# Sampling through the offsets phase: a gather table held twice, and six sample groups moved out of the first deform tiles

## What is computed

```python
x = x + _L0_conv_ref(_gn(x), ...)   # chunked linear attention, then group norm
x = x + _L1_conv_ref(_gn(x), ...)   # 3x3 conv gives per-pixel offsets; bilinear resampling; 3x3 conv
x = x + _L2_conv_ref(_gn(x), ...)   # 3x3 convolution
x = x + _L3_conv_ref(_gn(x), ...)   # deformable 3x3 convolution
```

## Time and profile before

| | us |
|---|---|
| median of 3 runs (11071.03 to 11081.85) | 11077.26 |
| profiled execution, span from first to last instruction | 11438.4 |
| mean granted TensorE clock in it, share of full | 0.775 |
| POOL busy, share of span | 6270.5 (55%) |
| PE busy, share | 6712.3 (59%) |
| DVE busy, share | 6213.1 (54%) |
| ACT busy, share | 2154.2 (19%) |

### The profile page before, as it was taken

The page is one execution under the profiler, slowest core; times in us unless marked ns, Lnnn a source line. Parts: engine busy times, 40 slices in busy tenths (PEclk is TensorE's granted clock), DMA queues, the critical chain, the costliest instruction groups (busy, mean ns, idle before and its releaser), DMA issues. The chain is left out here.

```text
span 11438.4 us, 98360 instructions
## 1 busy us (share of the span) xinstructions
PE 6712.3 (59%) x29196; PEld 4294.5 (38%) x29196; DVE 6213.1 (54%) x6833; ACT 2154.2 (19%) x3660; POOL 6270.5 (55%) x5206
## 2 busy tenths in 40 slices
PE   5455777656667677755676595756576583121212
PEld 3223336544454235534454234634454331111111
DVE  6797324566784524466795424466696433333333
ACT  2331311221221311122130221121221130000000
POOL 0000006578776406668876504668876605777777
PEclk8777888878888788877888797878788796555555
DMA  0000112222232312222223212222223222333333
GB/s 25 17 0 17 55 52 84 91 88 87 82 94 79 99 42 91 82 92 87 86 77 95 93 40 95 86 92 86 87 77 97 81 62 77 97 98 97 98 97 90
DMA packets 426636, 878.37 MB, mean 77 GB/s; under 512 B 119692, under 2 KB 250134, under 8 KB 423444
## 3 DMA queue, kind: packets, MB, share of 16 engines
q0 software_dynamic: 248832, 679.81, 20.1%
q1 hardware_dynamic: 174228, 121.56, 3.7%
q10 hardware_dynamic: 3456, 75.50, 1.6%
HBM read 764.88 MB, written 111.60 MB: 77 GB/s over the span
## 5 line engine op out<-in xcount | busy, mean ns | idle before, releaser
L589 POOL DMA_INDIRECT gathered_corners<-gather_table,metas x5184 | 6262.2, 1208 | 5143.2 <-issue 3134.3
L1212 PE MATMUL ps<-ident,weighted_corners 128*128 128x128 f32 (+1 forms) x10800 | 1590.1, 314 | 579.1 <-DVE weighted_corners L646 554.4
L1212 PEld LDWEIGHTS ps<-ident,weighted_corners 128*128 128x128 f32 (+1 forms) x10800 | 1500.6, 216 | 756.3 <-issue 584.9
L1215 PE MATMUL ps<-ident,sampled 128*128 128x128 f32 (+1 forms) x1530 | 370.6, 401 | 2407.1 <-DVE sampled L653 2399.6
L648 DVE TENSOR_TENSOR gathered_corners<-gathered_corners,metas 128x2304 f32<-128x2304 f32 x306 | 783.1, 2559 | 1665.3 <-DMA gathered_corners<-gather_table,metas 1603.8
L1016 ACT COPY sampled_by_channel<-ps 128x512 f32<-128x512 f32 x576 | 337.1, 585 | 5722.1 <-PE ps L1215 2688.5
L1286 PE MATMUL ps<-region,woff 128*128 (+1 forms) x3456 | 1222.7, 511 | 23.6 <-ACT region L1001 23.6
L1215 PEld LDWEIGHTS ps<-ident,sampled 128*128 128x128 f32 (+1 forms) x1530 | 248.2, 194 | 2552.0 <-issue 2438.7
L820 DVE TENSOR_TENSOR work<-work 128x768 f32<-128x768 f32 x960 | 888.3, 953 | 17.1 <-ACT work L1079 11.1
L646 DVE TENSOR_TENSOR weighted_corners<-gathered_corners,metas 128x2304 f32<-128x2304 f32 x270 | 690.9, 2559 | 340.6 <-DMA gathered_corners<-gather_table,metas 186.1
L1286 PEld LDWEIGHTS ps<-region,woff 128*128 128x128 f32 x3456 | 674.8, 199 | 516.2 <-issue 87.5
(11 more groups left out here) (205 smaller groups left out, 7276.9 us busy)
## 6 DMA issues: line engine op xcount, KB each, us to landing
gathered_corners<-gather_table,metas POOLq DMA_INDIRECT x5184
x_after_layer<-region ACTq DMA_DIRECT2D x8, 4608.0 KB, 12.3
gather_table<-tabst SPq DMA_DIRECT2D x192, 192.0 KB, 2.5
region<-in_x_dram ACTq DMA_DIRECT2D x12, 1536.0 KB
region<-x_after_layer ACTq DMA_DIRECT2D x4, 4608.0 KB, 16.6
res<-x_after_layer SPq DMA_DIRECT2D x144, 128.0 KB
out_dram<-ob SPq DMA_DIRECT2D x144, 128.0 KB
indices_and_weights<-region SPq DMA_DIRECT2D x16, 810.0 KB, 4.2
```

The costliest lines, as they stand in the source:

```text
L589: pool.indirect_dma_start(out=G[:, s % NG, k, :], out_offset=None, in_=table, in_offset=bass.IndirectOffsetOnAxis(ap=idx[:, s * KK + k:s * ...
L1212: mm = pe.matmul(out_m, W[:, q, 128 * m:min(128 * m + 128, KK * C)], ident[:, :], start=q == 0, stop=q == 3)
L1215: mm = pe.transpose(out_m, V[:, s % 2, 128 * m:min(128 * m + 128, KK * C)], ident[:, :])
```

## The change

- The table in DRAM is twice as long. Pass p writes the half p % 2 and the sampling of pass p reads the other, so that sampling may go on while the table is written. `first_row` (one number on each partition) holds the base of the indices and is flipped between the halves at the end of each pass. `setup()` zeroes the whole second half with two stores of 98 x 99 rows of 512 bytes each, ahead of the border stores on SP.
- The first six deform tiles carry one group each instead of two, by the schedule of the second six (PLACES[1]).
- The six groups taken away are sampled in the offsets phase: PARTS is 6, a part is 4 tiles and one group. PE does a step behind each tile, DVE weighs the four steps (summing on DVE), then does the part's indices and weights (now on 216 columns), then `finish`. SP's loads and stores of the group stand between the cosine loads, and its stores of the parts' indices and weights (six now) come after the last group's result is stored.

```diff
-PARTS = 4
+PARTS = 6
...
-G_TAPS = (G_NORM + 1, G_NORM + 1 + 12)
+G_TAPS = (G_NORM + 1, G_NORM + 1 + 6)
 G_CONV = (G_TAPS[1] + 6, G_TAPS[1] + 10)
-assert G_CONV[1] + 4 == GROUPS
+G_OFFSETS = G_CONV[1] + 4
+assert G_OFFSETS + PARTS == GROUPS
...
 PLACES = {0: ((), (), (), (), (), ()),
-          1: (((0, 0),), (), ((0, 1),), ((0, 2),), ((0, 3),), ((0, None),)),
-          2: (((0, 0), (0, 1)), ((0, 2),), ((0, 3),), ((0, None), (1, 0), (1, 1)), ((1, 2), (1, 3)), ((1, None),))}
+          1: (((0, 0),), (), ((0, 1),), ((0, 2),), ((0, 3),), ((0, None),))}
...
-DVE_SUMS = {1: (), 2: ((0, 1), (1, 1), (1, 3))}
...
-        table = dram("gather_table", (2 * TAB, 2 * C))
+        table = dram("gather_table", (2 * 2 * TAB, 2 * C))
...
+        first_row = sb("first_row", [128, 1])
...
-            tab4 = table.rearrange("(b h w) c -> b h w c", b=2, h=TAB_H)
+            tab4 = table.rearrange("(b h w) c -> b h w c", b=4, h=TAB_H)
             stores = []
+            for b in (2, 3):
+                stores.append((tab4[b], zero[0:TAB_H, 0:2 * C].unsqueeze(1).to_broadcast([TAB_H, TAB_W, 2 * C])))
...
+                    chain.own(chain.after().memset(first_row[:, :], float(TAB_W + 1)))
...
-            tiles_groups = (2, 1) if sample else (0, 0)
+            tiles_groups = (1, 1) if sample else (0, 0)
...
-            tabp = table.rearrange("(i h w) c -> i h w c", i=2, h=TAB_H)
+            if prepare:
+                tabp = table[bass.ds(p % 2 * (2 * TAB), 2 * TAB), :].rearrange("(i h w) c -> i h w c", i=2, h=TAB_H)
...
+                    sp.dma_start(metas[:, slot, :], meta_before[:, bass.ds(g * META, META)]).then_inc(meta_loaded[slot], 16)
...
+                def load_res(g):
+                    sp.dma_start(res[:, :], x3_before[:, bass.ds(g * GN, GN)]).then_inc(res_loaded, 16)
...
+                def store_out(g):
+                    sp.wait_ge(group_added, g + 2)
+                    sp.dma_start(out_before[:, bass.ds(g * GN, GN)], ob[:, :]).then_inc(out_stored, 16)
...
+                def group(g, e, last=False):
+                    load_res(g)
+                    if not last:
+                        sp.wait_ge(weighted, g * STEPS + CREDIT)
+                        load_meta(g + 1, 1 - e)
+                    store_out(g)
+
                 if sample:
...
+                    ahead = G_OFFSETS if prepare else GROUPS - 2
+                    with sp.Fori(0, ahead // 2) as j:
                         for e in range(2):
-                            group(j * 2 + e, e, False)
...
+                if not prepare:
+                    group(GROUPS - 2, 0)
                     group(GROUPS - 1, 1, True)
...
                     sp.wait_ge(out_stored, 16 * (GROUPS + 1))
-                if not prepare:
                     return
...
-                with sp.Fori(0, RT // 2) as j:
-                    for e in range(2):
...
-                        sp.wait_ge(om_mm, j * 2 + (e + 1))
...
+                def load_cosines(t, e):
+                    sp.wait_ge(om_mm, t + 1)
...
+                for h in range(PARTS):
+                    g = G_OFFSETS + h
+                    for u in range(4):
+                        load_cosines(h * 4 + u, u % 2)
+                        if sample and u == 1:
+                            if h > 0:
+                                store_out(g - 1)
+                            load_res(g)
+                            if g + 1 < GROUPS:
+                                sp.wait_ge(weighted, g * STEPS + CREDIT)
+                                load_meta(g + 1, (g + 1) % 2)
+                if sample:
+                    store_out(GROUPS - 1)
+                    sp.wait_ge(out_stored, 16 * (GROUPS + 1))
                 for h in range(PARTS):
...
-                                if e == 0:
-                                    steps_of(j * 2 + (G_TAPS[0] + gi), (G_TAPS[0] + gi) % 2, (s,), (gi, s) not in DVE_SUMS[2])
-                                else:
-                                    steps_of(j + G_TAPS[1], (j + G_TAPS[1]) % 2, (s,))
+                                steps_of(j + G_TAPS[e], (j + G_TAPS[e]) % 2, (s,))
...
                 with v.Fori(0, PARTS) as h:
+                    steps_of(h + G_OFFSETS, (h + G_OFFSETS) % 2, (0, 1, 2, 3), False)
                     v.wait_ge(om_tcp, h * (RT // PARTS) + (RT // PARTS + 2))
...
-                            ch.own(ch.after().tensor_scalar(idx, fl, float(TAB_W), float(TAB_W + 1), ALU.mult, ALU.add))
+                            ch.own(ch.after().tensor_scalar(idx, fl, float(TAB_W), first_row[:, :], ALU.mult, ALU.add))
...
                     ch.named(ch.after().tensor_tensor(wts[:, :, :, 0], half(q2), half(fl), ALU.subtract), meta_made, h + 1)
+                    steps_of(h + G_OFFSETS, (h + G_OFFSETS) % 2, (None,))
                     ch.restart()
+                ch.own(ch.after().tensor_scalar(first_row[:, :], first_row[:, :], -1.0, float(2 * (TAB_W + 1) + 2 * TAB), ALU.mult, ALU.add))
+                ch.after()
...
-                                steps_of(j * 2 + (G_TAPS[0] + gi) if e == 0 else j + G_TAPS[1], (s,))
+                                steps_of(j + G_TAPS[e], (s,))
...
+                        steps_of(h + G_OFFSETS, (u,))
                     mask(h)
...
+                    steps_of(GROUPS - 1, (u,))
                 mask(PARTS - 1)
...
-                            steps_of(j * 2 + (G_TAPS[0] + gi) if e == 0 else j + G_TAPS[1], (s,), (gi, s) not in DVE_SUMS[2 - e])
+                            steps_of(j + G_TAPS[e], (s,))
...
                 offsets_and_mask(0, 0, 0)
-                with pe.Fori(0, RT // 2 - 1) as j:
-                    offsets_and_mask(j * 2 + 1, 1, j)
-                    turn_offsets(j * 2, 0)
-                    offsets_and_mask(j * 2 + 2, 0, j + 1)
-                    turn_offsets(j * 2 + 1, 1)
-                offsets_and_mask(RT - 1, 1, RT // 2 - 1)
-                turn_offsets(RT - 2, 0)
-                turn_offsets(RT - 1, 1)
+                with pe.Fori(0, PARTS - 1) as h:
+                    for u in range(4):
+                        offsets_and_mask(h * 4 + (u + 1), (u + 1) % 2, h * 2 + (u + 1) // 2)
+                        turn_offsets(h * 4 + u, u % 2)
+                        steps_of(h + G_OFFSETS, (u,), False)
+                for u in range(4):
+                    t = RT - 4 + u
+                    if u < 3:
+                        offsets_and_mask(t + 1, (u + 1) % 2, (t + 1) // 2)
+                    turn_offsets(t, u % 2)
+                    steps_of(GROUPS - 1, (u,), False)
```

More of the change, by code:

```diff
@@ L488, in _, with load_meta @@
             def _(sp):
-                if sample:
[L491 to L500, removed]
+                def load_meta(g, slot):
+                    sp.dma_start(metas[:, slot, :], meta_before[:, bass.ds(g * META, META)]).then_inc(meta_loaded[slot], 16)
[10 more added lines that the diff above has]
+                    store_out(g)
+                if sample:
                     load_meta(0, 0)
-                    with sp.Fori(0, GROUPS // 2 - 1) as j:
+                    ahead = G_OFFSETS if prepare else GROUPS - 2
+                    with sp.Fori(0, ahead // 2) as j:
                         for e in range(2):
-                            group(j * 2 + e, e, False)
-                    group(GROUPS - 2, 0, False)
+                            group(j * 2 + e, e)
+                if not prepare:
+                    group(GROUPS - 2, 0)
                     group(GROUPS - 1, 1, True)
                     sp.wait_ge(out_stored, 16 * (GROUPS + 1))
-                if not prepare:
                     return
@@ L548, in _ @@
                 sp.wait_ge(cst_zeroed, 1)
-                with sp.Fori(0, RT // 2) as j:
-                    for e in range(2):
-                        sp.wait_ge(om_mm, j * 2 + (e + 1))
[L553 to L561, removed]
-                            src = cos_dram[k:k + 1, bass.ds((r0 + 1 - sy) * PAD2 + (1 - sx), run)]
-                            sp.dma_start(cst[e][q:q + 6].rearrange("p h w -> p (h w)"),
-                                         bass.AP(src.tensor, src.offset, [[1, 3], [4 * PAD2 * PAD2, 2], [1, run]])).then_inc(cs_loaded[e], 16)
+                def load_cosines(t, e):
+                    sp.wait_ge(om_mm, t + 1)
+                    r0 = t * ROWS
+                    run = cst[e][0:24].rearrange("p h w -> p (h w)").shape[1]
+                    src = cos_dram[:, bass.ds((r0 + 1) * PAD2 + 1, run)]
+                    sp.dma_start(cst[e][0:24].rearrange("p h w -> p (h w)"),
+                                 bass.AP(src.tensor, src.offset, [[1, 3], [PAD2 * PAD2, 8], [1, run]])).then_inc(cs_loaded[e], 16)
+                    for k, (sy, sx) in enumerate(DIRECTIONS):
+                        q = 24 + k * 6
+                        src = cos_dram[k:k + 1, bass.ds((r0 + 1 - sy) * PAD2 + (1 - sx), run)]
+                        sp.dma_start(cst[e][q:q + 6].rearrange("p h w -> p (h w)"),
```

(2 more changed lines are left out.)

## The result

The changed kernel takes **10492.5 us** (median of four runs, 10487.2 to 10495.9) against 11079.6 us for the kernel before, timed beside it: a ratio of 0.9469, 95% interval 0.9455 to 0.9482. The forecast was 10612 us (0.958), its range 10460 to 10790. The direction and the mechanism held; the gain is a quarter larger than forecast, 587 us where 465 were foreseen. One timed run among all that follow, of the kernel of experiment 8, took 15001 us beside three of 10903 to 10907, and the ratio there leaves it out.

The account below looks back on a forecast made before the run. No engine bounds the whole: POOL is overloaded in the first six deform tiles and idle in the PE-bound offsets phase. 3 x (134 - 300) - 3 + 21 takes 11438 to 10958, scaled to 10612 us; range 10460 to 10790.

Parts of the forecast that it names:

- first six tiles: Deform tiles 0 to 6 of a pass: six intervals fall from 695.0 to 395.2 us, -300 us a pass.
- offsets phase: After the cosines, POOL leads with the moved groups; the phase ends at 4389 instead of 4267.4, +122 us a pass.
- end of the pass: After the last result's store, six stores of indices and weights, 3.3 MB, take 13 us: +12 us a pass.
- setup, once: Zeroing 9.9 MB at 255 GB/s moves the next block's first issue from 60.1 to 81: +21 us, between nothing and +74.
- pass 0's phase, once: Offsets phase of pass 0, which has no sampling: its parts are smaller at the end, -3 us.
- The first part: Offsets phase: PE gives the fourth tile at about 4100, the second group's first weighing ends at 4118; POOL stands 22 us.
- The pace behind it: Offsets phase after the first part's lag: 18 steps x 13.2 + 4 x 3, 250 us, to 4368, ending at 4389.
- the 3 us a part: Offsets phase: DVE's index and weight work, 12.5 us a part, takes 3 us from POOL, making its sum 55.7.
- case 3: Waits between engines add up, index work blocks POOL fully: 65.2 us a group, +173 in the offsets phase; 10761 us; 20%.
- rival 1: POOL is never held up in the offsets phase: no first-part lag, indices free, +79; 10467 us; chance 13%.
- Case 4: TensorE's clock falls to its lower level and stays; PE leads the offsets phase at 80 us a part; 11089 us; 5%.
- Case 5: Setup's zeros go out through one DMA engine at 12.5 GB/s, 795 us; 11345 us; 7%, with other ways to lose.

Follow-up runs that it names:

- experiment 8: The changed kernel with each store that zeroes the second table half cut into 97 rows and 1 row, same bytes: 10906.2 us, ratio 0.984.
- experiments 2 and 4: 2: only the doubled table, on the kernel before, 11111.4 us; 4: the changed kernel with the second half's zeroing moved from setup to pass 0, 10467.9 us.
- experiment 5: The changed kernel with the zeroing moved to pass 0 and each part's indices and weights stored early, behind the next part's cosine loads: 10448.4 us, ratio 0.9428.
- experiment 1: The kernel before, unchanged, profiled a second time: 11080.6 us, ratio 1.0001, span 11079.7 us.
- experiment 7: The changed kernel with 14 convolution taps per tile instead of 9 in the offsets phase: 10685.1 us, ratio 0.9642.

## Why the prediction was right, and what it mis-sized

Point by point, pass 1, second profile of before against the changed kernel, in us:

| step | foreseen | measured |
|---|---|---|
| first six tiles | -300 | 692.2 to 393.3: -299 |
| from the normalization ahead of the tiles to tile 0 | none | 73.5 to 63.6: -10 |
| offsets phase | +122 | 232.9 to 327.5: +95 |
| end of the pass | +12 | 45.1 to 52.7: +8 |
| setup, once | +21 | 87.7 to 109.0: +21 |
| pass 0's phase, once | -3 | 232.5 to 229.0: -3.5 |

With the means of the three passes, -9.0, -299.3, +95.5 and +8.2 make -204.6 a pass, -614 in three; with +21, -4 in pass 0's phase, -2 in its attention and some +6 in the last pass that is -593, and the spans differ by 591.9.

**Tiles: right.** "The same program as the second six" gave 395 and the chip 393.3.

**Offsets phase: the mis-sized term,** 26.5 us a pass too dear, 80 in all. The timeline splits it into two halves.
- The first part. I had the second group's first weighing end 83.5 us after the cosines; it ended at 70.5 (3692.02 + 4.8 - 3626.3). The order in "PE gives the fourth tile only after five tiles and three transposes" was right; the time put on it, 57 us from PE's start at about 4043, was not. It took 41 us, from 3637.7 to DVE's 3678.57. The first tile's nine taps lie behind PE before the cosines come: already in the earlier trace rows the wait of 27.15 us stands ahead of L1371, the cosine weights, and not of L1367. The four tiles behind it, each with its turn and one step's transposes, follow every 9.4 us, at a granted clock of 0.97 for 3638 to 3679, where I had 10 for a tile and 1.3 for the transposes. The lag is real, but POOL stands for 14.5 us, not 22. PE's timeline, the cosine products of tiles 0, 1 and 4:

```profile
3637.68 3.54 PE L1397 MATMUL ps<-work,wcs 128*54 128x384 f32 x6 [26.30 <-DMA work<-cosines]
...
3646.86 2.10 PE L1397 MATMUL ps<-work,wcs 128*54 128x384 f32 x6
...
3674.98 2.10 PE L1397 MATMUL ps<-work,wcs 128*54 128x384 f32 x6
```

- The pace behind it. I had the remaining way to the end at 271 us and it took 257, 2.7 less for each of five groups. A group takes 52.6 us instead of 55.7 and some waiting. The term that was wrong is the 3 us a part that DVE's index work was to take from POOL, at the weighing's rate of 1.8 per 4.8 us. The timeline of part 1 shows what it took. Here are the start of a weighing and the gathers beside it and beside the index work, which runs from 3730.09 to 3742.50, 12.4 us:

```profile
3725.10 2.56 DVE L670 TENSOR_TENSOR gathered_corners<-gathered_corners,metas 128x2304 f32<-128x2304 f32 x1 [6.93 <-DMA gathered_corners<-gather_table,metas]
3725.93 2.54 POOL L611 DMA_INDIRECT gathered_corners<-gather_table,metas  x1 [0.30 <-issue]
...
3728.78 1.09 POOL L611 DMA_INDIRECT gathered_corners<-gather_table,metas  x1 [0.30 <-issue]
...
3730.17 1.01 POOL L611 DMA_INDIRECT gathered_corners<-gather_table,metas  x1 [0.30 <-DVE sampled L675]
...
3742.84 0.95 POOL L611 DMA_INDIRECT gathered_corners<-gather_table,metas  x1 [0.30 <-issue]
```

The ten gathers from 3730.17 to 3742.84 come every 1.267 us, where bare ones come every 1.25: the index work costs POOL 0.2 us a part, not 3. The delay does not grow with DVE's busy time. A gather is held once, at its start, by the one instruction that DVE is in then: it ends 0.82 us after that instruction (3725.10 + 2.56 is 3727.66, the gather ends at 3728.47). In this trace that is so for 305 of the 308 gathers that began inside an L670, and for all 296 that began inside an L672, the first of the adds. L670 is long (2.56 us) and costs this gather 1.6, the add behind it costs the next one 0.15, and that is the 1.8 us of a weighing; an index instruction lasts 0.2 to 0.6 us and costs at most 0.08. Not every instruction does it: beside the reduction L829, with one input, and L729, one of whose two inputs lies in PSUM, the gather stays at 0.95; the copy L981 out of SBUF does hold it, to 1.01. The Trainium skill (SBUF, "Who interferes with whom") says that a DVE instruction with two SBUF inputs contends with a GpSimd instruction that reads SBUF; the prediction gave that without its condition on the GpSimd side. The gather reads its indices in `metas`, and the numbers above agree with the rule, gather by gather. What does not follow is case 3's reading, that the index work as a whole would hold POOL.

So POOL leads, as forecast, with nearly the free index work of rival 1 behind the first part and a shorter lag than the forecast's in it. The phase and the end of the pass add 104 us, where rival 1 had 91 and the forecast 134: the result, 10492, lies 25 us above rival 1's 10467 and 120 below the forecast. Rival 1 left out the 21 us of setup, which experiments 2 and 4 show to be exposed.

**Ahead of tile 0: a term I did not see.** The first place of a tile stands before its marker, and with two groups a tile it held two steps. DVE's timeline ahead of tile 0 in pass 1, in the second profile of before:

```profile
2251.40 2.56 DVE L646 TENSOR_TENSOR weighted_corners<-gathered_corners,metas 128x2304 f32<-128x2304 f32 x1
...
2259.18 2.56 DVE L648 TENSOR_TENSOR gathered_corners<-gathered_corners,metas 128x2304 f32<-128x2304 f32 x1 [5.22 <-DMA gathered_corners<-gather_table,metas]
...
2264.03 0.28 DVE L813 TENSOR_REDUCE small<-ps 1x1 f32<-1x128 f32 x1
```

and in the changed kernel:

```profile
2266.77 2.56 DVE L668 TENSOR_TENSOR weighted_corners<-gathered_corners,metas 128x2304 f32<-128x2304 f32 x1 [0.28 <-DVE small L829]
2269.37 0.28 DVE L832 TENSOR_REDUCE small<-ps 1x1 f32<-1x128 f32 x1
```

The second step, its 5.22 us of waiting for a gather and its 4.8 of weighing are gone. Counting from the first marker hid 27 us in three passes: an interval measured between markers leaves out what lies ahead of the first one.

**End of the pass:** 12 foreseen, 8.2 measured (mean of three passes), 11 in all; experiment 5 shows that the late burst of stores is the whole of it, since issuing them early brings the stage to 42.5, below the 45.1 of before.

**The ratio.** The sum, -480, was made against a profile with 360 us in it that the runs do not have, and then scaled by 11077 / 11438. By experiment 1 the extra time lies where the change does nothing, so the difference should have been carried over whole: 11077 - 480 = 10597, 15 nearer. These four (80, 27, 11, 15) are 133 us, against the miss of 120; the last pass's +6 and the scatter of the runs lie between them.

**The rivals.** Case 3 leaned on the convolution's 65.5 us a group and 52 us of waits, both from the first profile: in the second it is 58 and 25, and its other leg, index work that blocks POOL, is answered above. Case 4 did not come: granted 0.89 in the window above. Case 5 is shown possible by experiment 8, at a lower price than it had, and was avoided by 98 rows. As an estimate from experiment 7, PE takes over from POOL when its tiles take some 35 us more in the phase than today.

## What to carry to other kernels

Move work to where the engine it needs is idle, and price it by what it adds there: a group that cost 50 us beside another group on the same engine cost 18 where that engine had nothing. Most of the 18 is what six groups need beyond the work that was there: room is used up after about four. To price what one engine's work costs another, look at the one instruction that it meets, not at the sum of busy times. Measure a stage from the last point that the change leaves alone, not from the first marker inside it. If one profile is longer than the runs, profile the same kernel again before scaling by it.

## What the runs showed of the hardware

A store of 97 rows of 99 x 512 bytes moves at 22 GB/s, one of 98 rows at about 240. A gather (`DMA_INDIRECT`) that started inside a weighing's multiplication ended 0.82 us after it, in 305 of 308 cases; 12.4 us of short index instructions delayed ten gathers by 0.2 us together. One profiled execution was 3% longer than the timed runs, with the extra time in some stages only and with waits that no engine of the core ends; its cause was not found.
